# A fused Flamingo block on one core: whole-row first load, fewer root steps, routing logits as bf16 halves, another place for the last gate, and last stores in quarters

## The reference

```python
x = x + tanh(g_xattn) * attention(layernorm(x), ctx, ctx, mask)   # 32 heads, 8 groups, D = 64
h = layernorm(x)
query = h @ Wq.T                                   # 64 wide
router = (query @ Wr.T) @ (aux_keys @ Wr.T).T / sqrt(48) + log_rel
top8 = top_k(router, 8)                            # of 512 slots
w = softmax(query @ aux_keys.T / sqrt(64) + log_rel, over the top8 slots)
aux = (w @ aux_values) @ Wvd.T @ Wvu.T
learned = gelu(h @ Wu1.T + bu1) @ Wu2.T + bu2
u = clip(0.5 * log1p(var(h)) / mean(log1p(var)) + 2.5 * sigmoid(learned), 0, 5)
gate = sigmoid(gate_w1 * clip((u - 0.5) / 1.5, 0, 1) + gate_bias), 0 where under 0.05
x = x + tanh(g_ffn) * (h + gate * aux)
```

## Time and profile before

| | us |
|---|---|
| three timed executions | 1220.26, 1217.95, 1216.82 (median 1217.95) |
| the profiled execution's own time | 1217.31 |
| its span | 1215.1 |
| TensorE busy | 1177.3 (97%) |
| VectorE busy | 987.3 (81%) |
| ScalarE busy | 890.3 (73%) |
| GpSimd busy | 901.8 (74%) |
| moved by DMA | 94.70 MB, mean 78 GB/s |

### The profile page before, as it was taken

One profiled execution on the slowest core, in us unless ns is written; L12 is line 12 of the kernel. 1 busy time (PEld: TensorE's weight loads), 2 busy tenths in 40 slices (PEclk: granted clock), 3 DMA queues, 4 the chain that ended last, 5 costly groups with the idle time before them and its releaser, 6 DMA issues.

```text
span 1215.1 us, 35246 instructions
## 1 busy us (share of the span) xinstructions
PE 1177.3 (97%) x14642; PEld 916.3 (75%) x14642; DVE 987.3 (81%) x2224; ACT 890.3 (73%) x1209; POOL 901.8 (74%) x850
## 2 busy tenths in 40 slices
PE   5999999999999999999999999999999999999997
PEld 3888888888888888888888888888877555555553
DVE  5897899889889988998998899888883776676564
ACT  4888888888888888888888888888862345554443
POOL 5999999999999899999999989998960023222423
PEclk9999999999999999999999999999999999999998
DMA  9421223141223213121312231131237100122112
GB/s 313 117 78 44 60 73 88 40 99 34 82 57 95 76 40 92 54 78 44 93 43 85 56 83 41 40 79 47 68 95 253 80 1 1 70 105 87 53 70 104
DMA packets 60225, 94.70 MB, mean 78 GB/s; under 512 B 35170, under 2 KB 44386, under 8 KB 55972
## 3 DMA queue, kind: packets, MB, share of 16 engines
q1 hardware_dynamic: 59924, 92.45, 25.4%
q10 hardware_dynamic: 144, 0.00, 0.0%
HBM read 71.36 MB, written 20.97 MB: 76 GB/s over the span
## 4 chain that ended last, share of the span: by engine, by line
PE 80%; ACT 8%; DVE 6%; POOL 3%; issue 2%; DMA 1%; SPq 0%; DVEq 0%; POOLq 0%
PE psum L847 13%; PE psum L870 13%; PE psum L923 11%; PE psum L877 8%; PE psum L858 6%; PE psum L900 6%; PE psum L894 5%; PE psum L895 5%; PE psum L1002 3%; ACT arena L687 2%; ACT arena L683 2%; PE psum L825 2%; PE psum L910 2%; PE psum L938 2%; POOL arena L571 1%
## 5 line engine op out<-in xcount | busy, mean ns | idle before, releaser
L571 POOL TENSOR_TENSOR arena<-arena 128x768 bf16<-128x768 f32 x448 | 652.6, 1470 | 58.5 <-ACT arena L683 42.0
L1225 DVE CUSTOM_DVE_ANT_0 arena<-psum,arena 128x750 f32<-128x750 f32 x448 | 420.1, 938 | 83.9 <-PE psum L858 76.8
L687 ACT ACTIVATE arena<-arena,neg_max 128x750 f32<-128x750 f32 x448 | 410.6, 916 | 65.5 <-DVE neg_max L1225 65.5
L683 ACT ACTIVATE arena<-psum 128x768 f32<-128x768 f32 x320 | 258.4, 808 | 65.2 <-PE psum L877 63.0
L847 PE MATMUL psum<-arena 128*128 128x512 bf16 x896 | 272.8, 385 | 0.0
L870 PE MATMUL psum<-ident,arena 128*128 128x128 f32 x1792 | 269.0, 273 | 0.0
L894 PEld LDWEIGHTS psum<-arena 128*128 128x128 bf16 (+1 forms) x2688 | 194.6, 98 | 57.5
L895 PE MATMUL psum<-arena 128*128 128x64 bf16 (+1 forms) x2688 | 222.0, 193 | 0.0
L894 PE MATMUL psum<-arena 128*128 128x65 bf16 (+1 forms) x2688 | 221.6, 194 | 0.0
L895 PEld LDWEIGHTS psum<-arena 128*128 128x128 bf16 (+1 forms) x2688 | 178.5, 98 | 53.2
L870 PEld LDWEIGHTS psum<-ident,arena 128*128 128x128 f32 x1792 | 206.7, 140 | 4.3
(11 more groups left out here) (144 smaller groups left out, 1441.4 us busy)
## 6 DMA issues: line engine op xcount, KB each, us to landing
arena<-in_k_t SPq DMA_DIRECT2D x128, 187.5 KB, 3.2
out<-arena SPq DMA_DIRECT2D x13, 1024.0 KB, 3.8
arena<-in_v_rows SPq DMA_DIRECT2D x64, 192.0 KB, 2.5
arena<-in_x_top SPq DMA_DIRECT2D x7, 1024.0 KB, 6.0
arena<-in_x_rest SPq DMA_DIRECT2D x8, 768.0 KB, 5.3
spill<-arena SPq DMA_DIRECT2D x96, 64.0 KB, 2.2
arena<-spill SPq DMA_DIRECT2D x6, 1024.0 KB, 7.3
arena<-in_w_t SPq DMA_DIRECT2D x4, 1024.0 KB, 20.8
```

Source lines behind the costliest of these rows:

```text
L571: pool.tensor_tensor(p_lo[:, n % RING, :], p_sb[:, n % RING, :], high(p_sb[:, n % RING, :]), ALU.subtract).then_inc(p_split, 1)
L683: act.activation(p_sb[:, n % RING, :], flat_ps[:, turned_at(n):turned_at(n) + CW], ACT.Copy).then_inc(evac_a, 1)
L687: act.activation(s_sb[:, n % RING, 0:CTX], s_sb[:, n % RING, 0:CTX], ACT.Exp, bias=neg_max[:, n % 4, :], scale=-1.0).then_inc(exped, 1)
L1225: dve.tensor_tensor_reduce(s_sb[:, n % RING, 0:CTX], flat_ps[:, score_at(n):score_at(n) + CTX], mask_sb[:, max(n % UNITS - REP + 1, 0), :] ...
```

## The change

- The first 128 rows are loaded whole, in one transfer; the wait of the statistics is for all of them. The step "times 1/8" goes: the variance plus epsilon is multiplied by 64 in the same GpSimd instruction before the power.
- VectorE splits the first query block ahead of the three small steps between the two averaging matmuls.
- At the boundary each `turn_h(1, j)` moves one or more steps later, and the router table's matmul comes ahead of the second wide product.
- The keys table is loaded twice, into both halves of the partitions, and split into two bf16 tables (`keys_hi` by ScalarE in window 2, `keys_lo` by GpSimd at the boundary, after a scaling pass). The query is split too (`query_hi` on ScalarE, `split_query` on VectorE, stacked as `q_cat`). The logits are now two bf16 products. `log_rel` is added from a table of rows on VectorE, and a masked sum with a minimum takes the place of the maximum.
- The last tile's gate leaves GpSimd's list: two exps on ScalarE and eight column steps and a product on VectorE, with one add of the tile before between the two halves of the chain. GpSimd keeps only the inverse of the weights' sum for it.
- The last two tiles are stored in quarters of a row, even ones by SyncE, odd ones by ScalarE.

```diff
-            for c in range(4):
-                sp.dma_start(xa[:, 0, 512 * c:512 * c + 512], x_top[0, :, 512 * c:512 * c + 512]).then_inc(first_top_loaded[c], 16)
+            load_top(0)
             load_rest(0)
...
-            for dst, src in (..., (keys_aug[0:BOT, :], keys_t)):
+            for dst, src in (..., (keys_raw[0:BOT, :], keys_t), (keys_raw[BOT:128, :], keys_t)):
...
-            for u in ORDER[:-1]:
+            for u in ORDER[:-2]:
                 sp.wait_ge(y_added, parts_before(u, 4))
                 sp.dma_start(out[u], rows_of(u)).then_inc(out_stored, 16)
...
+            for u in ORDER[-2:]:
+                for n in (0, 2):
+                    sp.wait_ge(y_added, parts_before(u, n + 1))
+                    sp.dma_start(out[u, :, 512 * n:512 * n + 512], rows_of(u)[:, 512 * n:512 * n + 512]).then_inc(out_stored, 16)
```

```diff
-                pool.tensor_tensor(ln_ve[:, cols], ln_mv[:, cols, 1], ln_eps[:, cols], ALU.add).then_inc(ln_ve_done, 1)
+                pool.tensor_scalar(ln_ve[:, cols], ln_mv[:, cols, 1], EPS, float(D), ALU.add, ALU.mult).then_inc(ln_ve_done, 1)
+
+            def factors(i, cols):
                 pool.wait_ge(ln_ve_done, i + 1)
-                pool.tensor_tensor(ln_rstd[:, cols], ln_ve[:, cols], ln_half[:, cols], ALU.pow).then_inc(ln_rstd_done, 1)
...
-                pool.tensor_tensor(ln_scale[:, cols], ln_rstd[:, cols], ln_eighth[:, cols], ALU.mult).then_inc(ln_scale_done, 1)
+                pool.tensor_tensor(ln_scale[:, cols], ln_ve[:, cols], ln_half[:, cols], ALU.pow).then_inc(ln_scale_done, 1)
...
+            pool.wait_ge(keys_hi_done, 1)
+            pool.wait_ge(rk_summed, 1)
+            pool.tensor_scalar(keys_raw, keys_raw, float(BOT) ** -0.5, None, ALU.mult).then_inc(keys_split, 1)
+            pool.wait_ge(keys_split, 1)
+            pool.tensor_tensor(keys_lo[:, :], keys_raw, keys_hi[:, :], ALU.subtract).then_inc(keys_split, 1)
```

```diff
+            def query_hi(t):
+                act.wait_ge(q_ready, t + 1)
+                if t >= 1:
+                    act.wait_ge(routed, t)
+                act.activation(q_cat[0:BOT, :], q_aug[0:BOT, :], ACT.Copy).then_inc(q_cat_hi, 1)
...
                 pe.matmul(psum[:, 4, :], q_aug, rk_aug, start=True, stop=True)
-                pe.matmul(psum[:, 5, :], q_aug, keys_aug, start=True, stop=True).then_inc(routed, 1)
...
+                pe.wait_ge(q_cat_done, t + 1)
+                pe.matmul(psum[:, 5, :], q_cat, keys_hi[:, :], start=True, stop=False)
+                pe.matmul(psum[:, 5, :], q_cat, keys_lo[:, :], start=False, stop=True).then_inc(routed, 1)
...
+            def split_query(t):
+                dve.wait_ge(q_cat_hi, t + 1)
+                dve.tensor_tensor(q_cat[BOT:128, :], q_aug[0:BOT, :], q_cat[0:BOT, :], ALU.subtract).then_inc(q_cat_done, 1)
...
-                dve.scalar_tensor_tensor(w_rows, w_rows, -1.0e30, psum[:, 5, :], ALU.mult, ALU.add).then_inc(logits_done, 1)
+                dve.scalar_tensor_tensor(w_rows, w_rows, -1.0e30, rel_rows, ALU.mult, ALU.add).then_inc(logits_done, 1)
                 dve.wait_ge(logits_done, t + 1)
-                dve.tensor_reduce(neg_top[:, :], w_rows, AX.X, ALU.max, negate=True).then_inc(selected, 1)
+                dve.tensor_tensor_reduce(w_rows, psum[:, 5, :], w_rows, -1.0, 3.4e38, ALU.add, ALU.min, neg_top[:, :]).then_inc(selected, 1)
```

```diff
+            act.wait_ge(dotted, TILES)
+            act.activation(last_col[:, 0:1], learned[:, TILES - 1:TILES], ACT.Exp, bias=scal_neg[:, 3:4], scale=-1.0).then_inc(last_exped, 1)
             round_z(TILES - 1)
+            store_quarter(TILES - 2, 1)
+            act.wait_ge(last_clipped, 1)
+            act.activation(last_col[:, 4:5], last_col[:, 3:4], ACT.Exp, bias=scal_neg[:, 2:3], scale=scal_neg[:, 1:2]).then_inc(last_exped, 1)
+            store_quarter(TILES - 2, 3)
+            store_quarter(TILES - 1, 1)
+            store_quarter(TILES - 1, 3)
...
             split_z(TILES - 1)
-            for i in range(2, 8):
+            dve.wait_ge(last_exped, 1)
+            last(dve.tensor_scalar(column(1), column(0), 3.0e38, 1.0, ALU.min, ALU.add))
+            last(dve.reciprocal(column(2), column(1)))
+            last(dve.tensor_scalar(column(1), column(2), 2.5 / (TAU_HIGH - TAU_LOW), norm_var[:, TILES - 1:TILES], ALU.mult, ALU.add))
+            dve.tensor_scalar(column(3), column(1), 0.0, 1.0, ALU.max, ALU.min).then_inc(last_clipped, 1)
+            finish(TILES, 2)
+            dve.wait_ge(last_exped, 2)
+            last(dve.tensor_scalar(column(5), column(4), 3.0e38, 1.0, ALU.min, ALU.add))
+            last(dve.reciprocal(column(6), column(5)))
+            last(dve.scalar_tensor_tensor(column(5), column(6), EARLY_EXIT, column(6), ALU.is_ge, ALU.mult))
+            dve.wait_ge(factor_ready, 1)
+            last(dve.tensor_tensor(aux_scale[:, TILES - 1:TILES], column(5), column(7), ALU.mult))
+            for i in range(3, 8):
                 finish(TILES, i)
```

The order of TensorE's steps at the boundary:

```diff
             turn_h(0, 2)
             turn_h(0, 3)
             sum_query(0, 0)
-            turn_h(1, 0)
...
             sum_wide(0, 1)
             sum_query(0, 1)
-            turn_h(1, 1)
+            turn_h(1, 0)
...
             sum_query(0, 2)
-            turn_h(1, 2)
+            turn_h(1, 1)
             sum_v2(range(2, 4))
             sum_wide(0, 3)
             sum_query(0, 3)
+            turn_h(1, 2)
+            sum_v2(range(4, 6))
             turn_h(1, 3)
-            sum_v2(range(4, 6))
             route(0)
             sum_v2(range(6, 8))
```

92 lines of the change are left out of this document (57 added, 35 removed).

## The result

The kernel after takes 1206.97 us (median of four runs, 1206.29 to 1207.09). The kernel before takes 1217.38 us (median of four, 1216.36 to 1220.26: the three executions above and one more). The ratio is 0.9911, 95% interval 0.9896 to 0.9926, so 10.4 us are gained. The profiled execution took 1206.96 us with a span of 1205.2, where before it was 1217.31 and 1215.1.

The account below looks back on a forecast made before the run. TensorE was taken to bound attention and mostly feed-forward, other engines and transfers both ends. Start 0.3 + boundary 1.4 + tiles 4.5 + end 3.3 = 9.5 us, giving 1208 us (1206 to 1209.5 at chance 0.52; range 1204 to 1212).

Parts of the forecast that it names:

- (d): Rival: transfers give way at start and boundary, first load lands at 5.3; gains 1.2 + 2.8 + 5.0 + 3.8, 1204.7 us; chance 0.12.
- The start: Opening of the kernel: first product of scores at 15.0 instead of 15.32 us, 0.3 gained, between -0.5 and 1.2.
- The row of steps: Opening: query halves ready near 13.1, split until 13.6, small steps 0.75, matmul 0.6, so scores at 15.0 us.
- the first scores' 0.3: Opening: the earlier scores' gain, kept although waits for the third window's keys could take it back; 0 if the backlog stayed.
- The boundary: Between attention and feed-forward: the 2.35 us wait goes, transfers become late next, tile loop starts 1.4 us earlier (0.4 to 2.8).
- the transfers' gap: Boundary: earlier weight pieces free their slots sooner, closing the one gap in the stream of transfers, worth about 1 us.
- The tiles: Route of each tile: one fp32 product becomes two bf16 ones, 0.43 us less TensorE time each; 4.5 us gained (1.5 to 5.6).
- The hand-off: Route of each tile: after the join, ScalarE copies and VectorE subtracts to make the query's halves, 0.63 us with two hand-offs.
- Rival (a): Route of each tile: the hand-off eats its gain; an exchange of 1.2 us leaves 1.5 at most, 1211 us; chance 0.15.
- rival (b): Route of each tile: slower than before, starting at a hand-off of about 1.9 us; 1222 us at 2.4; chance 0.03.
- The end: Last tiles: gate on ScalarE and VectorE gains 2.9 us, quarter stores 0.4; together 3.3, between 1.8 and 4.0.
- Rival (c): Last gate: table load waits for the score, column steps take 0.35 us; the end gives 1.5 or 1.1, 1210.0 us; chance 0.14.

Follow-up runs that it names:

- hi_twice: The kernel after, with ScalarE's copy of each query's first bf16 half made twice, the first into a tile nobody reads: 1206.80 us.
- start_only: The kernel before with only the changed opening: whole first load, shorter root, first query split ahead of the three small steps: 1217.37 us.
- quarter_load: The kernel after with the first row loaded in four column quarters again, everything else kept: 1206.33 us.
- before_again: The kernel before, unchanged, profiled a second time: 1219.02 us.
- warm_before: The kernel before with 70 unused transposes of the identity added on TensorE before its first real work: 1218.90 us.
- split_late: The kernel after with the first query split moved back behind the three small steps: 1205.05 us.
- pieces_first: The kernel after with the three loads of the running state issued behind all weight pieces: 1203.66 us.
- boundary_old: The kernel after with TensorE's and ScalarE's order at the boundary as in the kernel before, SyncE's order kept: ratio 0.9936.
- pieces_halves: The kernel after with state loads behind all weight pieces, and stores as before (whole row, then two halves, on SyncE's queue): 1205.19 us.

## Why the prediction was right, and where it was not

**The total.** Predicted 1208, measured 1206.97, inside the range of 1204 to 1212 and faster, as forecast. Against the profile, 9.5 predicted and 9.9 measured in span. None of the rivals happened. Of (d) the tiles reached their 5.0 and the start went past its 1.2, but the boundary and the end stayed under its 2.8 and 3.8.

**The start: mechanism half right, size wrong (0.3 against 2.7).** The row of steps came out as predicted, to the product of scores at 15.0. The step that failed is the silent one behind it: that the time of the first product is what attention starts from. I compared the starts of the masked maximum's read-out (L1225 before, L1260 after) unit by unit. The kernel after leads by 0.32 us in the first unit, by 1.73 at 28 us, 2.04 at 46, 2.55 at 118 and 2.72 at the end. So three things come on top, of 1.4, 0.3 and 0.7 us.
First, TensorE's products are long at the start and become short at a moment that differs between executions. A pair of 512 columns takes 1.06 us in the long form and 0.60 in the short. The last long pair starts at 17.98 in the kernel after, and at 21.70 in hi_twice, which is the same kernel up to there:

```profile
17.98 1.06 PE L881 MATMUL psum<-arena 128*128 128x512 bf16 x2
...
20.82 0.61 PE L881 MATMUL psum<-arena 128*128 128x512 bf16 x2
```

```profile
21.70 1.06 PE L883 MATMUL psum<-arena 128*128 128x512 bf16 x2
...
24.34 0.60 PE L883 MATMUL psum<-arena 128*128 128x512 bf16 x2
```

Their ends of attention differ by 1.5 us. The clock's record gives the moment itself: 18.98 in the kernel after, 23.98 in hi_twice. Of eight profiles with the start of the kernel after (start_only among them), the four with the rise at 18.4 to 21.5 us have a start worth 2.4 to 3.0, and the four with the rise at 23.1 to 24.0 one of 1.2 to 1.7. So some 1.2 us of the 2.7 belong to the execution. Whether the early load makes the early rise likelier stays open: all four profiles with quarter loads have it at 23.8 to 24.1, nine of the ten with whole-row loads earlier than that, which leans to yes, but four are few, and quarter_load's median is no worse.
Second, the third window's keys. The prediction kept the first scores' 0.3 on the ground that the backlog might move; it moved by more than its own 0.83 us of wait: DMA share from 36 to 38 us is 0.12 (before 1.02), and neither GpSimd nor TensorE waits. That is worth 0.3 on TensorE. quarter_load, whose keys are waited for 1.01 us, loses 0.2 there.
Third, 0.5 us between 100 and 115 us and 0.2 more between 200 and 340. The half microsecond is gained in one step behind 112 us, where this wait of the kernel before has no counterpart after; its other two waits around it, 0.33 and 0.24 us, became 0.57 and 0.23:

```profile
111.93 0.44 PE L877 MATMUL psum<-ident,arena 128*128 128x128 f32 x2 [0.41 <-ACT arena L683]
```

Every profile with the new root has these 0.7 us, and neither before_again nor warm_before has them. The runs separate the edit: start_only has the three edits of the opening alone, quarter_load lacks the load, split_late the early split, and all show the same steps, so what they share, GpSimd's shorter root, is the cause. How it takes the wait away is not shown. The prediction priced the root for the opening only and said that between 60 and 900 us the change has almost nothing. It is all of quarter_load's 0.7.

**The boundary: right place, and in the profiled execution the wrong sign (1.4 predicted, -0.9 measured).** The wait of 2.35 us went, and the next late thing was a weight piece, as predicted; it was the fifth, at 925.57, not the seventh and eighth near 933. The step that failed has two parts. I took the transfers' gap as the only slack, and did not look at which loads stood ahead of the pieces: with the state loads behind them the whole 2.8 is there (pieces_first). And I priced a wait as a wait. Behind the stall of 1.86 us the granted clock was 0.50 from 926.93 to 930.34, which made 3.7 us of products into 5.5.
The -0.9 is one execution's, though. Five profiles have this order of TensorE with the kernel after's order of loads, and their boundaries are worth -0.9, 0.5, 1.2, 1.7 and 1.9 us; the middle one is near the 1.4. The other three executions of the kernel after have a mean clock of 0.999, where the profiled one has 0.998, so they probably had no fall at the boundary, and they took the same time. What made them as long wasn't profiled. The new order still pays against the old one, through the executions in which the old one loses its clock (boundary_old's median is 2.7 us longer).

**The tiles: right (4.5 against 5.1).** One fp32 product of 0.87 us became two of 0.22, 0.43 per tile. In the routes' starts the gain is 0.43 in tile 1, 0.20 and 0.23 in tiles 2 and 3, and 0.43 in each of the ten others, where the prediction had 0.36, 0.06, and 0.35 to 0.43. Two terms were too small: VectorE's extra work in tiles 2 and 3 showed less than the sum of its parts, and the wait of 0.41 us in tiles 6 to 9 did not eat its share. The hand-off was sized well: from the join's start to the difference's end 0.94 us, with 0.66 after the join, for the predicted 0.63; TensorE's wait in tile 2 grew from 0.74 to 1.19, predicted 1.1. Rival (a) and rival (b) fall with these rows, the exchange being 0.66 us and not 1.2 or more, and with hi_twice: more hand-off costs in the two tiles without slack and little elsewhere.

**The end: right (3.3 against 3.0).** The table load started ahead of its operand and cost 1.30 us to the exp, the column steps took 0.14 to 0.21 us at a pace of 0.2, and the five last adds start 4.1 us after the last fp32 product (8.3 for four adds in the kernel with GpSimd's gate). Rival (c) is out. One sign was stated wrongly: last adds "from about 6 us after the last score reduction" doesn't follow from the sum, which has them at 1205.7 with the score at 1201.6, 4.1 us; they came 3.5 us after it (1194.64 to 1198.13). Where I put 2.9 on the gate and 0.4 on the stores, the runs show that the two can't be added in either order: the gate alone is worth 2.4 (pieces_halves), the stores alone nothing, both 3.0. The 0.4 was my estimate from the size of the last store alone, and no run separates size from the second queue: the quarters moved no faster together than the halves did (311 GB/s from 1202 to 1204 us in the kernel after, 403 from 1199 to 1202 in pieces_halves), they only started sooner (the first store of the last two rows at 1191.51 in pieces_first, at 1196.69 in pieces_halves).

**The chances.** 0.52 went to a case that holds its time but not its shares; the range was held through errors of 2.4 and 2.3 us with opposite signs, both in stretches that come out otherwise in other executions. That part was luck.

## What to carry to other kernels

When a stall is taken out, look in the queue of transfers at what stands ahead of the next thing that will be late: loads that are needed 10 us later belong behind it, and that one edit was worth 3.3 us here. Price a stall of the matrix engine not by its length alone but with what its clock may do behind it (here 0.50 for 3.4 and 6.8 us in two profiles), and sort the executions by their mean granted clock before comparing medians: start_only's gain of 1.9 to 2.7 us was visible only so. And where executions differ, compare cuts of the traces stretch by stretch before believing a difference of medians; of the pairs here with nearly equal medians, three had a stretch that differed by 0.6 to 2.1 us.

## What was unexpected in the hardware

A wait of TensorE of about 2 us was followed by half the clock or not, for the same length: 2.35 us was followed by a granted clock of 0.50 in start_only and of 1.00 in both profiles of the kernel before and in boundary_old; 1.86 us by 0.50 in the kernel after, 1.40 by 1.00 in hi_twice. It costs 1.7 us behind the 1.86, and about 3.2 behind the 2.35, which is more than the wait.

The granted clock's column says nothing before the trace's first record of the clock. In the kernel before, that record is the rise at 24.1 us; the column shows 1.00 from 18 to 24 us, where pairs of products take 1.06 us, and in warm_before, whose record starts at 7.0, it shows 0.50 for the same durations. The durations of like products are the surer sign.

A clock that had risen held while TensorE mostly idled: in warm_before the granted clock stayed at 1.00 from 7.0 to 17.2 us although TensorE was busy for only 1.3 of the four us from 12 to 16.

Quarter stores of 256 KB (2 KB for each partition) on two queues moved 311 GB/s at the end of the kernel after (1202 to 1204 us), where the halves moved 395 in the kernel before (1212 to 1214 us): the smaller pieces started sooner here, and were not moved as fast. Whether their size or the second queue does it, no run separates.
